# One DMA transpose for each 16-bit part of a head's exponentials, the high part issued ahead of GpSimd's low part

## The reference

```python
s = jnp.einsum('bhid,bhjd->bhij', q, k) * SCALE     # 512 queries x 512 keys (508 and 4 in the first)
p = jax.nn.softmax(s, axis=-1)
o = jnp.einsum('bhij,bhjd->bhid', p, v)             # head width 64
```

## Time and profile before

| | us |
|---|---|
| runs | 1254.41, 1253.20, 1248.27; median 1253.2 |
| profiled execution, its own time | 1245.08 |
| its span | 1243.3 |
| PE, ACT, DVE, POOL busy | 950.8, 757.0, 724.9, 649.8 |
| granted PE clock, mean | 0.898 |
| first attention's loop | about 128 to 564 |
| second attention's loop | about 885 to 1108 |

### The profile page before, as it was taken

The page is one execution under the profiler, slowest core; times in us unless marked ns, Lnnn a source line. Parts: engine busy times, 40 slices in busy tenths (PEclk is TensorE's granted clock), DMA queues, the critical chain, the costliest instruction groups (busy, mean ns, idle before and its releaser), DMA issues. The chain is left out here.

```text
span 1243.3 us, 24205 instructions
## 1 busy us (share of the span) xinstructions
PE 950.8 (76%) x9167; PEld 734.3 (59%) x9174; DVE 724.9 (58%) x1302; ACT 757.0 (61%) x1265; POOL 649.8 (52%) x563
## 2 busy tenths in 40 slices
PE   3976789899989989985515999907778888961675
PEld 3755567676767667764414999905456666751344
DVE  2553557657655766654274444456466665638776
ACT  2453868868876887881433444304678787834576
POOL 1330856767675667670376555303467676733122
PEclk9988999999999999996656999958899999975889
DMA  9740999999998999992342222144499899962001
GB/s 261 275 170 6 184 185 178 178 210 159 178 184 172 158 182 155 156 169 52 119 143 85 73 82 73 56 144 173 79 181 166 158 156 158 165 103 101 5 26 39
DMA packets 444193, 171.01 MB, mean 138 GB/s; under 512 B 410128, under 2 KB 427728, under 8 KB 444048
## 3 DMA queue, kind: packets, MB, share of 16 engines
q1 hardware_dynamic: 440336, 159.23, 64.1%
q0 software_dynamic: 3744, 10.23, 2.6%
HBM read 49.68 MB, written 19.05 MB: 55 GB/s over the span
## 5 line engine op out<-in xcount | busy, mean ns | idle before, releaser
L467 POOL TENSOR_TENSOR A_PHL<-A_pr,A_PHL 128x508 f16<-128x508 f32 x256 | 295.3, 1158 | 171.3 <-ACT A_pr L772 171.0
L977 DVE TENSOR_REDUCE A_negmax<-A_ps 128x2 f32<-128x1016 f32 x128 | 155.4, 1214 | 75.7 <-PE A_ps L605 75.2
L467 POOL TENSOR_TENSOR C_PHL<-C_pr,C_PHL 128x512 f16<-128x512 f32 x128 | 148.3, 1165 | 89.4 <-ACT C_pr L772 89.0
L771 ACT ACTIVATE A_PHL<-A_ps,A_negmax 128x508 f16<-128x508 f32 x256 | 179.6, 701 | 20.2 <-DVE A_negmax L977 19.2
L772 ACT ACTIVATE A_pr<-A_ps,A_negmax 128x508 f32<-128x508 f32 x256 | 181.3, 708 | 0.0
L623 PE MATMUL A_ps<-A_VH,A_PT 128*128 128x65 bf16 (+1 forms) x1024 | 109.6, 197 | 38.1 <-DMA A_PT<-A_PHL 37.9
L623 PEld LDWEIGHTS A_ps<-A_VH,A_PT 128*128 128x128 f16 (+1 forms) x1024 | 93.7, 98 | 66.7 <-DMA A_PT<-A_PHL 54.3
L605 PE MATMUL A_ps<-A_K,A_Q 64*128 64x508 f32 x768 | 124.5, 429 | 11.1 <-ACT A_pr L772 9.0
L624 PE MATMUL A_ps<-A_VL,A_PT 128*128 128x64 f16 (+1 forms) x1024 | 108.8, 194 | 0.0
L625 PE MATMUL A_ps<-A_VH,A_PT 128*128 128x65 bf16 (+1 forms) x1024 | 108.6, 195 | 0.0
L977 DVE TENSOR_REDUCE C_negmax<-C_ps 128x2 f32<-128x1024 f32 x64 | 78.2, 1222 | 43.0 <-PE C_ps L605 42.8
(11 more groups left out here) (353 smaller groups left out, 2740.2 us busy)
## 6 DMA issues: line engine op xcount, KB each, us to landing
A_PT<-A_PHL SPq DMA_TRANSPOSE x256, 3.4
M_rin<-in_L_ffn_w_in SPq DMA_DIRECT2D x8, 512.0 KB, 3.7
M_rout<-in_L_ffn_w_out SPq DMA_DIRECT2D x8, 512.0 KB, 4.0
M_WINh<-M_parts SPq DMA_DIRECT2D x32, 128.0 KB, 2.6
C_CT<-ct_split SPq DMA_DIRECT2D x5, 768.0 KB, 5.1
v_high<-A_VH SPq DMA_DIRECT2D x12, 260.0 KB, 2.1
A_VH<-v_high SPq DMA_DIRECT2D x12, 260.0 KB, 3.2
v_low<-A_VL SPq DMA_DIRECT2D x12, 256.0 KB, 2.7
```

The lines of the kernel that those rows point to most:

```text
L467: pool.tensor_tensor(PHL[:, e % PRING, 1, 0:KEYS], pr[:, e % RING, 0:KEYS], PHL[:, e % PRING, 0, 0:KEYS], ALU.subtract).then_inc(pl_ready. ...
L771: a.activation(PHL[:, e % PRING, 0, 0:KEYS], o, ACT.Exp, bias=nm[:, n % 4, h:h + 1])
L977: v.tensor_reduce(nm[:, g % 4, :], ps[:, S_BANK + 2 * (g % 2):S_BANK + 2 * (g % 2) + 2, 0:KEYS], AX.X, ALU.max, negate=True).then_inc(max_ ...
```

## The change

Each head's tile is transposed by two DMA instructions instead of one. The first takes the high part (512 elements of a row, four blocks) and waits for ACT's `p_ready`; the second takes the low part and waits for POOL's `pl_ready`. The full count of `pt_loaded` for a step is therefore 64 and not 32, here and in the two places that wait for it. POOL's clearing of the pad columns now raises `cleared`, and SP waits for it ahead of its first transpose, as does PE ahead of its first scores.

```diff
-        cleared = sem("cleared", 3)
+        cleared = sem("cleared", 4)
...
-        pt_loaded = [sem(f"pt_loaded{k}", 32 * G // PTS) for k in range(PTS)]
+        pt_loaded = [sem(f"pt_loaded{k}", 64 * G // PTS) for k in range(PTS)]
...
+            wait(sp, cleared, 4 if ipa else 1)
             for n in range(G):
                 b, u = n // U, n % U
                 if n >= PTS:
                     wait(sp, pv_done, n - PTS + 1)
                 for h in range(2):
                     e = 2 * n + h
+                    wait(sp, p_ready, e + 1)
+                    sp.dma_start_transpose(out=PT[n % PTS][:, h, 0:QT, :], in_=PHL[:, e % PRING, 0, :]).then_inc(pt_loaded[n % PTS].sem, 16)
                     wait(sp, pl_ready, e + 1)
-                    sp.dma_start_transpose(out=PT[n % PTS][:, h, :, :],
-                                           in_=PHL[:, e % PRING, :, :].rearrange("p s n -> p (s n)")).then_inc(pt_loaded[n % PTS].sem, 16)
+                    sp.dma_start_transpose(out=PT[n % PTS][:, h, QT:2 * QT, :], in_=PHL[:, e % PRING, 1, :]).then_inc(pt_loaded[n % PTS].sem, 16)
...
-                pool.memset(PHL[:, :, :, KEYS:N], 0.0)
+                pool.memset(PHL[:, :, :, KEYS:N], 0.0).then_inc(cleared.sem, 1)
...
-                wait(pe, pt_loaded[n % PTS], 32 * (n // PTS + 1))
+                wait(pe, pt_loaded[n % PTS], 64 * (n // PTS + 1))
...
-            wait(pe, cleared, 3 if ipa else 1)
+            wait(pe, cleared, 4 if ipa else 1)
...
-                    wait(a, pt_loaded[n % PTS], 32 * (n // PTS))
+                    wait(a, pt_loaded[n % PTS], 64 * (n // PTS))
```

## The result

| | before | changed |
|---|---|---|
| runs, us | 1254.41, 1253.20, 1248.27, 1252.24 | 1648.10, 1653.70, 1651.52, 1657.30 |
| median, us | 1252.72 | 1652.61 |
| ratio, 95% interval | | 1.3216 (1.3165 to 1.3267) |
| span of the profiled execution, us | 1243.3 | 1646.3 |
| granted PE clock, mean | 0.898 | 0.813 |

The changed kernel is 400 us slower. The page of the changed kernel gives busy time by engine and the slices of PE and of the DMA share; these answer to the earlier trace rows.

What follows compares the result with a forecast made beforehand. Prediction: PE and the exponentials-to-transposed-tile path near their limit, SP's issue dense; 40 + 16 (queueing) + 5 (unevenness) + 3 (V loads) = +64 us on 1245.1 gave 1309, plus 8 to the runs' median 1317 us; range 1212 to 1400.

Steps and rivals of the forecast that it cites:

- The bound before: Attention loops: PE and the path from exponentials to transposed tile near their limit, SP dense at 2.65 of 3.41 us a step.
- One of half the size costs SP 0.87 us: SP's issue of a half-size transpose: part fixed as in plain copies, the rest halved, 0.87 us, bounds 0.62 to 1.23.
- rival (c): SP's issue of a half-size transpose all fixed or nearly, 1.0 to 1.23 us: 1403 to 1600 us; chance 0.12.
- A step keeps SP for 3.72 us: SP in the attention loops: four issues of 0.87 us with 0.06 us gaps, 3.72 us a step against 2.74 before.
- The sum by stretches: Attention loops cut into 27.25 us stretches: steps times 3.72 less 27.25, where positive, adds 40 and 16 us.
- The earlier landing: Last transpose of a step, where SP is free: the low half lands earlier, at most 1.25 us off 3.0 to 3.4.
- PE gains nothing from the early high part: PE's first matmul of a step waits for both halves of both heads, so only the last landing counts; no gain.
- The pad wait: SP and PE waiting for POOL's clearing of pad columns, done at 83.0 us, before the first transpose at 124.0: 0 us.
- the packets: Transposes' DMA packets: data packets unchanged, only the 16 completion packets double; 0 us if hidden, at most 8 us.
- SP's waits for POOL: SP's waits for POOL's low parts in the first attention, 84.7 us before, were to be nearly gone.

Runs made afterwards that it cites:

- a step of slack: The kernel before with `LAG` 4 in place of 3, the weighing four steps behind the scores: 1216.1 us, 0.9706 of before.
- the sizes run: The kernel before with 20 transposes of ten shapes added, each issued alone at the end of SP's second attention: 1288 us.
- The three-issue run: The kernel before with head 0 of each pair still transposed whole and head 1 in two parts: 1422.7 us, 1.1416 of before.
- late start: The changed kernel with both halves waiting for POOL's low part: 1656.6 us, 1.3303 of before.
- the regrouped kernel: The kernel before with one transpose for both heads' high parts and one for both low parts, two issues a step: 1244.8 us, 0.9961 of before.

## Why the prediction was wrong

The direction was right; the time, 1317 us with a range up to 1400, was not. Step by step:

- *The bound before.* Half right. The bytes were none, shown by the run with half of them (3.2%), and SP's stream was the one to look at: half as many issues again (three a step) cost 14%. But it was close to a bound and not yet one: one issue a step freed it and gained nothing, with LAG 3 or 4, while a step of slack, which leaves it as it is, gained 3%.
- *One of half the size costs SP 0.87 us.* Wrong, and the step that failed. It was 1.26 us, just above the upper end of my bounds, 1.23; that end alone, in rival (c)'s sum, gives 283 of the 336 us that were missing. I took the plain copies' 0.43 to 0.58 us as the fixed part of any DMA's issue, and gave the rest of the transpose's 1.23 us to its blocks. The sizes run shows that this rest is fixed too: 1.13 us for a single block of 128 x 128. What misled me is the choice of the nearest row: a copy is another instruction, and that its issue doesn't depend on size was itself a hint that issues on this queue are priced by kind. A second hint stood in the rows and was given to rival (c) only: no byte moved in the first 1.1 us of an issue.
- *A step keeps SP for 3.72 us.* The form, four times issue and gap, was right: 4 x (1.26 + 0.05) = 5.24 us measured in the dense stretches, 5.16 for rival (c).
- *The sum by stretches.* With rival (c)'s 5.16 it gave 1600 us, measured 1653. It reckoned with the shortest issue, 1.23 us, where the mean of the 768 is 1.31: 60 us, of which 42 are what 53 stretched issues (up to 2.7 us) last beyond the median. The mean step of the first loop is 717.5 / 128 = 5.6 us, loads included. Taking the median, 1.33, for the whole ones likewise overstated SP's room before: the working has SP used for 2.65 of 3.41 us a step, under 80%, and puts 121 us of waits beside it, where the stream fills 90% and the idle gaps of the first loop are 38 us. The three-issue run, 1423 where the same method gave 1370 to 1390, errs the same way: a stream at its limit gives back none of its irregularities.
- *The earlier landing.* The half landed in 2.5 us in the median, 0.9 less than the whole's 3.4; I had up to 1.25. The estimate by the Trainium skill ("DMA: Bandwidth & Descriptors", "Anatomy of one DMA", a fit for GpSimd's queue), 0.3 us less for 128 KB less, was too small beside it; the sizes run shows 0.6 us in isolation (3.09 against 2.47). It had no effect that shows, since SP was late anyway.
- *PE gains nothing from the early high part.* Right, as far as the runs can tell: late start against early start differ by 0.9%, at most by 1.8%, and the regrouped kernel, which has the early start for nothing, gains 0.4%.
- *Small terms.* The pad wait and the packets cost nothing that shows, though an extra transpose brought 32 packets and not 16 (440336 on the page's hardware queue before, 452624 after, for 384 more). SP's waits for POOL didn't vanish from the view as I said they would (84.7 to 78.0 us), for it counts them over SP's own work; the idle gaps of the first loop did, 38 to 2 us.
- *Chances.* Rival (c) held 0.12. The terms gave ends of 0.62 and 1.23 us with no row of a second transpose size, and I put most of the weight in the middle. With no row inside the interval the ends deserved more.

## What to carry to other kernels

Before an instruction of a queue is doubled, sum that queue's own instructions, mean duration (not the median) by count, against the loop's time; the engine table doesn't list it. Such a stream can be nearly full without setting the pace, and have next to no room for more. Without a row of the same instruction at another size, take its issue as fixed, and think of merging or of more slack (here one constant, 3%) rather than of cutting. Whether a wait for a DMA is latency or throughput the view doesn't tell; more slack does, and so do the gaps in the issuing queue.

## What the runs showed of the hardware

- A DMA transpose occupies SP for 1.11 to 1.23 us from 16 rows x 1024 or 128 x 128 up to 128 x 1024 elements of 16 bits, where a copy of 256 KB takes 0.43. Only at 512 KB does it grow: 1.9 us alone, 1.3 at the least and 2.1 in the median in the loop. Why stays open.
- Stretched issues coincide with something else than data. In the changed kernel the window 222.5 to 224.8, which holds the issue of 2.13 us, has one packet of the instruction queue:

```profile
DMA packets 1004, 0.27 MB, mean 115 GB/s; under 512 B 1003, under 2 KB 1003, under 8 KB 1003
...
q8 instruction: 1, 0.02, 2.6%
```

  The 16 us before it, with twelve issues of ordinary length, have none. The page counts 76 such packets in both kernels. Over the whole trace of the changed kernel, 46 of the 53 issues that last over 0.3 us more than the median have such a packet begin during them or in the 0.3 us ahead of them, of the other 715 issues 26. That an engine's code is fetched then, and holds up the transpose that is being issued, is an inference from this coincidence.
- PE's granted clock fell from 0.98 and 0.95 in the two loops to 0.82 and 0.80, a mix of the levels 2.4 and 1.2 GHz, as PE's busy share fell from 0.89 to 0.68 in the first. It cost nothing that shows, since PE waited for SP in any case and SP was idle for 3 us only.
